# A routed expert layer on one core: VectorE's loop without a placed head, and forty increments ahead of TensorE's stream

## The chip, the cores and the metric

The kernel runs on one core of one Trainium2 chip. The number that counts is the device time of one execution in microseconds (us), from the first instruction of the program to its last wait, as the median of several executions. A profiled execution is one of them with every instruction and DMA packet recorded.

## What is computed

The input is x of 64 batches by 64 channels by 512 (4096 rows, "tokens", of 512). A first product mixes the 64 channels of a batch by a matrix chosen by the batch's subject and adds a bias. The result h goes through a mixture of experts, and the sum is added to x:

```
h      = einsum('bct,bcd->bdt', x, w[subject]) + bias[subject]
scores = sigmoid(h @ gate.T)                 # 16 experts in 4 groups
sel, w = best 4 experts out of the best 2 groups (by scores + expert_bias)
w      = 2.5 * scores[sel] / sum(scores[sel])
out    = sum over the 4 chosen e:  w_e * (silu(h @ g_e.T) * (h @ u_e.T)) @ d_e.T
shared = (silu(h @ gs.T) * (h @ us.T)) @ ds.T
x      = x + out + shared                    # H = 512, inner size I = 256
```

## The kernel before, in words

**Stages.** The rows are cut into 32 tiles of 128. In a first stage TensorE forms h (line 1031, two tiles at a time out of four 64x64 pieces each), turns it (line 982) and forms the gate's logits (line 1008). In the second stage it computes the shared expert for all 32 tiles (lines 1144 to 1171), while VectorE works out the routing: which tokens go to which expert and in which of 143 tiles of 128 slots. In the third stage, the longest, the 143 routed tiles follow each other: GpSimd gathers a tile's rows by an indirect DMA, SyncE's DMAs rearrange them, VectorE transposes them, and TensorE does twelve matmuls into psGU (gate and up), two transposes of the product of the tile before, and six matmuls into psY (down) of the tile before that (function step, line 1215). Every weight and activation is split into a high and a low fp32r part, so a product is three matmuls. ScalarE takes the silu and the high parts, VectorE the mix by the routing weight (line 1758) and the low parts (lines 1749 and 1677), ScalarE copies psY out, and GpSimd scatters it, adding to the output.

**What sets the order.** Each engine has its own list of instructions, written out by hand, and engines meet only at semaphores. For the routed tiles every engine but GpSimd has a loop, built by the function run_tiles: some tiles written out ahead of the loop (head), a loop whose body holds 16 tiles, and some written out behind it (tail). TensorE and ScalarE (the tuple FFN) have 13 tiles ahead, eight turns and 2 tiles behind; VectorE and SyncE (the tuple EARLY) have 16 ahead, seven turns and 15 behind. All loops ask for a hint on their closing branch, which is given at the top of each turn.

**TensorE's beginning.** It waits for two memsets, runs eight warm-up matmuls on a tile of ones (line 968), waits for the constants (line 969) and goes on with the first pair of h tiles and the bias. A similar device, semaphore increments that nobody waits for, stands in SyncE's list (SP_STEPS, lines 502 and 503).

Of the kernel before, what the change touches and what calls it, by code (L numbers as in the profile page):

```python
# [83 lines left out]
GROUP = 4  # L84
RAW_LOADS = {15: 1, 16: 2, 23: 3, 31: 4}
WARM_UP = 8
DVE_HEAD = 77
SP_STEPS = 6
N_PAIRS = NT // 2
LATE_CONSTS = range(3, 8)  # L90
EIGHT = 8
# [28 lines left out]
def tile_at(n):  # L120
    return Tile(n // RING, n % RING)

def run_tiles(eng, first, head, rounds, tail, step, slot=None):

    for n in range(first, first + head):
        step(tile_at(n), n, n - first)
    start = first + head
    unroll = 2  # L130
    with eng.bass.Fori(0, rounds // unroll, engines=[eng.engine], hint_back_edge=True,
                      head_slot=None if slot is None else {eng.engine: slot}) as turn:
        for j in range(unroll * RING):
            step(Tile(turn * unroll + (start + j) // RING, (start + j) % RING), None, j)
    start += RING * rounds
    for n in range(start, start + tail):
        step(tile_at(n), n, n - start)

def build(nc, x, x_pairs, itok, fside, cond_w, gate_w, expert_bias, ffn_w, out):  # L140
# [4 lines left out]
    with ExitStack() as ctx:  # L145
# [6 lines left out]
        def sem(name):  # L152
            return ctx.enter_context(nc.semaphore(name))
# [134 lines left out]
        first = in_x([E, NRP])  # L288
# [85 lines left out]
        pads_cleared = sem("pads_cleared")  # L374
        scatter_ok = sem("scatter_ok")
        sp_clear = sem("sp_clear")
        act_clear = sem("act_clear")
        dve_clear = sem("dve_clear")
        shuffled = [sem(f"shuffled{s}") for s in range(RING // DUO_TILES)]
# [15 lines left out]
        EARLY = (NT, 2 * RING, TURNS - 2, NR - RING * TURNS)  # L395
# [101 lines left out]
        def _(sp):  # L497
# [3 lines left out]
            sp.dma_start(fside2[:], fside).then_inc(fside_loaded, 16)  # L501
            for _ in range(SP_STEPS):
                sp.sem_inc(sp_clear, 1)
# [5 lines left out]

            for m in range(N_PAIRS):  # L510
                if m + X_PAIRS < N_PAIRS:
                    sp.wait_ge(cond_done, 2 * (m + 1))
# [89 lines left out]
            for n in range(NT):  # L602
                step(tile_at(n), n, n)
            run_tiles(sp, *EARLY, step)
            for s in range(YRING):
                sp.wait_ge(scattered[s], 16 * ((NT + NR + YRING - 1 - s) // YRING))

        @block.gpsimd
        def _(pool):
# [50 lines left out]
            word = None  # L660
            for m in range(N_PAIRS):
                if m == 1:
# [69 lines left out]
        def _(act):  # L732
# [42 lines left out]
            def copy_h(n):  # L775
                act.wait_ge(cond_done, n + 1)
                if n >= H_RING:
                    act.wait_ge(h_stored[n % H_RING], n // H_RING * 16)
                    act.wait_ge(a_xposed, n + 1 - H_RING)
                act.activation(h_row(n), h_bank(n)[:], ACT.Identity,  # L780
                               bias=bias_tok[:, n:n + 1]).then_inc(h_ready, 1)

            def keep_xT(n):
                if n == DVE_COPIES:
                    act.wait_ge(a_xT_ready, DVE_COPIES)
                act.wait_ge(a_xposed, n + 1)
                act.activation(kept_xT(n), psT[n % 2][:], ACT.Copy).then_inc(a_xT_ready, 1)
# [6 lines left out]

            for m in range(N_PAIRS + 1):
                pair = (2 * m, 2 * m + 1)
                if m < N_PAIRS:
                    for n in pair:
                        copy_h(n)
                if m == N_PAIRS:  # L800
                    keep_xT(NT - 2)
# [151 lines left out]
            for n in range(NT):  # L953
                shared_step(n)
            run_tiles(act, *FFN, step)
            act.wait_ge(down_done, LAST - 1)
            for k in range(IK):
# [7 lines left out]
        def _(pe):  # L965
            pe.wait_ge(blank, 2)
            for _ in range(WARM_UP):
                pe.matmul(psM[:, 0:P], ones[:], ones[:], start=True, stop=True)  # L968
            pe.wait_ge(consts, 1)

            def bias():
# [270 lines left out]
            def last_downs(w, last_w):  # L1242
# [19 lines left out]
                mm.then_inc(down_done, 1)  # L1262

            run_tiles(pe, *FFN, step)
            last_downs(kept[-2], kept[-1])

        @block.vector
        def _(v):
# [173 lines left out]
            used, not_last, start, end, turn, prep, prep_end = [e_rows[:, k, :] for k in range(7)]  # L1442
# [263 lines left out]
            def shared_step(n):  # L1706

                g, part = divmod(n, GROUP)
                more = g < NT // GROUP - 1
                if part == 0:  # L1710
                    if g > 0:
                        shared_mix(g - 1, 1)
                    else:
                        route_part(n)
                    if more:
                        split_shared_x(GROUP * (g + 1))
                    if g > 0:
                        split_shared_hid(g - 1, 0)
                        split_shared_hid(g - 1, 1)
                elif part == 1:  # L1720
                    if more:
                        split_shared_x(GROUP * (g + 1) + 1)
                    if g == 0:
                        route_part(n)
                    shared_mix(g, 0)
                elif part == 2 and more:
                    split_shared_x(GROUP * (g + 1) + 2)
                    split_shared_x(GROUP * (g + 1) + 3)
                if n > 1:
                    route_part(n)  # L1730
                if n in LOWS:
                    split_low(*LOWS[n])
                if n == NT - 2:
                    turn_x(tile_at(NT))
                elif n == NT - 1:
                    split_x(tile_at(NT))
                    turn_x(tile_at(NT + 1))
# [153 lines left out]
            first_word = []  # L1891
            for n in range(NT):
                shared_step(n)
            run_tiles(v, *EARLY, step, DVE_HEAD)
            for k in range(IK):
                v.wait_ge(hidhi_ready, LAST + 1 + k)
                v.tensor_tensor(last_hidT(hidT_lo, k), last_hid_bank(k), last_hidT(hidT_hi, k).bitcast(F32), ALU.subtract
# [48 lines left out]
```

## Time and profile before

| | |
|---|---|
| three executions | 825.04, 826.39, 826.95 us; median 826.39 |
| profiled execution, its own time | 826.33 us |
| its span, first to last instruction | 824.5 us |
| TensorE busy | 812.5 us, 99% |
| VectorE, ScalarE, GpSimd busy | 485.0, 388.3, 433.4 us |
| fetch queue of TensorE (q8) | 17 packets, 0.28 MB |
| fetch queue of the other engines (q14) | 150 packets, 1.23 MB |

In the profile PE is TensorE, PEld its weight loads, DVE VectorE, ACT ScalarE, POOL GpSimd and SP SyncE; a letter q behind a name is that engine's instruction queue (registers, branches, semaphores), whose work is not counted as busy. Matmuls are pipelined: the shown duration of one is longer than the distance to the next, so groups are compared by their starts. In a row of the timeline the brackets hold the idle time of the engine ahead of the group and what ended it; "issue" there means that nothing the profile shows was waited for. fp32 matmuls run as two passes and count twice.

### The profile page before, as it was taken

To read this page: it belongs to the slowest core of one execution; us is meant where nothing else is said; L and a number is where in the kernel's file an instruction comes from. 1 tells how busy PE (TensorE), PEld (TensorE's weight loads), DVE (VectorE), ACT (ScalarE), POOL (GpSimd) and SP (SyncE) were. 2 spreads that over 40 slices of the span, in tenths; PEclk is the share of its full clock that TensorE was granted. 3 is DMA by queue.
4 is the path that set the end of the run, shared out by engine and by line. 5 is a ranking of instruction groups with operands and counts; after the bars stand their busy time and mean duration, and the time that the engine had idled before them with its cause. 6 is when DMAs were issued, how large, how long until landed. Compare 5 with 4: busy or idle time off the path is not lost.

```text
span 824.5 us, 19365 instructions
## 1 busy us (share of the span) xinstructions
PE 812.5 (99%) x4133; PEld 649.7 (79%) x4134; DVE 485.0 (59%) x1017; ACT 388.3 (47%) x782; POOL 433.4 (53%) x399
## 2 busy tenths in 40 slices
PE   9999999999999999999999999999999999999996
PEld 5578778888887888888888888888888888888874
DVE  5798899627444446644457446647557466464441
ACT  4864334535334345534455445546455355453441
POOL 5403112625567555566665665655565573765543
PEclk9999999999999999999999999999999999999999
DMA  8986969899999899899997999899998998998965
GB/s 288 394 332 177 247 149 260 204 203 268 239 251 237 177 192 176 202 276 241 182 196 185 270 216 217 210 267 189 229 266 175 282 246 198 236 206 164 198 94 68
DMA packets 145305, 181.52 MB, mean 220 GB/s; under 512 B 30570, under 2 KB 103922, under 8 KB 142834
## 3 DMA queue, kind: packets, MB, share of 16 engines
q0 software_dynamic: 37776, 89.08, 52.3%
q1 hardware_dynamic: 106528, 80.45, 38.4%
q10 hardware_dynamic: 834, 10.49, 3.6%
q14 instruction: 150, 1.23, 0.5%
q8 instruction: 17, 0.28, 0.1%
HBM read 82.52 MB, written 67.17 MB: 182 GB/s over the span
## 4 chain that ended last, share of the span: by engine, by line
PE 93%; DVE 3%; issue 1%; DMA 1%; ACT 1%; POOLq 0%; POOL 0%; DVEq 0%; SPq 0%; ACTq 0%
PE psGU L1111 47%; PE psY L1111 23%; PE psY L1169 5%; PE psH L982 4%; PE psGU L1152 3%; PE psGU L1154 3%; PE psGU L1153 3%; PE psT L982 1%; DMA raw_w<-ffn_w 1%; PE psY L1031 1%; PE psGU L1031 1%; PE psH L1008 1%; PE psM L1139 1%; PE psM L968 0%; DVE aT_low L1703 0%
## 5 line engine op out<-in xcount | busy, mean ns | idle before, releaser
L1111 PE MATMUL psGU<-split_w,xT_pair 128*128 x1716 | 415.9, 391 | 1.0 <-issue 1.0
L1111 PEld LDWEIGHTS psGU<-split_w,xT_pair 128*128 128x128 f32 x1716 | 321.9, 188 | 71.7 <-issue 1.9
L694 POOL DMA_INDIRECT out<-y_ring,idx_all x143 | 228.8, 1600 | 203.6 <-SPq L583 184.1
L1758 DVE SCALAR_TENSOR_TENSOR aT<-aT,w_ring,psGU 128x256 f32<-128x256 f32 x143 | 68.6, 480 | 238.6 <-ACT aT L934 216.1
L689 POOL DMA_INDIRECT tok_ring<-h_rows,idx_all x143 | 150.3, 1051 | 73.3 <-issue 42.0
L1111 PE MATMUL psY<-split_w,hidT_hi 128*128 x564 | 187.9, 414 | 0.0
L934 ACT ACTIVATE aT<-psGU 128x256 f32<-128x256 f32 x143 | 55.0, 384 | 255.2 <-PE psGU L1111 255.2
L840 ACT ACTIVATE y_ring<-psY 128x512 f32<-128x512 f32 x173 | 103.6, 599 | 101.1 <-PE psY L1111 63.3
L1111 PE MATMUL psY<-split_w,hidT_lo 128*128 x282 | 111.4, 395 | 0.0
L1111 PEld LDWEIGHTS psY<-split_w,hidT_hi 128*128 128x128 f32 x564 | 95.4, 189 | 13.5 <-issue 0.2
L1743 DVE STREAM_TRANSPOSE psT<-x_ring 128x512 f32<-128x512 f32 x143 | 102.5, 717 | 0.1
L1677 DVE TENSOR_TENSOR xT_pair<-psT,xT_pair 128x512 fp32r<-128x512 f32 x143 | 97.4, 681 | 4.7 <-issue 2.6
L755 ACT ACTIVATE xT_pair<-psT 128x512 fp32r<-128x512 f32 x143 | 86.3, 604 | 0.8 <-DVE psT L1743 0.8
L702 POOL DMA_DIRECT2D out<-y_ring x32 | 29.6, 1169 | 91.4 <-ACT y_ring L840 90.1
L1771 DVE TENSOR_TENSOR split_w<-raw_w,split_w x42 | 51.5, 1226 | 33.3 <-ACT split_w L906 31.7
L1111 PEld LDWEIGHTS psY<-split_w,hidT_lo 128*128 128x128 f32 x282 | 52.8, 187 | 12.4
L1749 DVE TENSOR_TENSOR hidT_lo<-psH,hidT_hi 128x256 fp32r<-128x256 f32 x142 | 59.3, 417 | 4.0 <-ACT hidT_hi L831 4.0
L831 ACT ACTIVATE hidT_hi<-psH 128x256 fp32r<-128x256 f32 x142 | 53.8, 379 | 1.6 <-PE psH L982 1.6
L982 PE MATMUL psH<-ident,aT 128*128 128x128 f32 x284 | 54.0, 272 | 0.5 <-DVE hidT_lo L1749 0.5
L982 PEld LDWEIGHTS psH<-ident,aT 128*128 128x128 f32 x284 | 39.3, 139 | 19.2 <-DVE aT L1758 0.9
L906 ACT ACTIVATE split_w<-raw_w x42 | 44.6, 1061 | 7.3 <-issue 2.4
L1153 PE MATMUL psGU<-split_w 128*128 128x512 f32 x96 | 37.4, 390 | 0.0
(268 smaller groups left out, 651.4 us busy)
## 6 DMA issues: line engine op xcount, KB each, us to landing
x_ring<-tok_ring SPq DMA_DIRECT2D x284, 128.0 KB
raw_w<-ffn_w SPq DMA_DIRECT2D x17, 1536.0 KB, 10.1
out<-y_ring POOLq DMA_DIRECT2D x32, 256.0 KB, 7.5
x_ring<-x_pairs SPq DMA_DIRECT2D x12, 512.0 KB, 8.6
h_rows<-tok_ring SPq DMA_DIRECT2D x16, 256.0 KB, 9.7
h_rows<-y_ring SPq DMA_DIRECT2D x16, 256.0 KB, 10.0
tok_ring<-h_rows,idx_all POOLq DMA_INDIRECT x143, 6.5
out<-y_ring,idx_all POOLq DMA_INDIRECT x143, 6.2
```

The lines of the kernel that those rows point to most:

```text
L689: pool.indirect_dma_start(tok_ring[:, r % RING, :], None, h_rows[:, :], bass.IndirectOffsetOnAxis(idx_all[:, r:r + 1], 0)).then_inc(gather ...
L694: pool.indirect_dma_start(out[:, :], bass.IndirectOffsetOnAxis(idx_all[:, r:r + 1], 0), y_ring[:, r % YRING, :], None, compute_op=ALU.add) ...
L755: act.activation(xT_hi[:, t.slot % 2, :], psT[t.slot % 2][:], ACT.Copy).then_inc(xhi_ready, 1)
L840: act.activation(y_ring[:, s, :], psY[t.slot % 2][:], ACT.Copy).then_inc(y_ready, 1)
L934: act.activation(silu[:, t.slot % 2, :], psGU[t.slot % 2][:, 0:I], ACT.Silu).then_inc(silu_ready, 1)
L982: mm = pe.transpose(dst[:, k * P:(k + 1) * P], src[:, k * P:(k + 1) * P], ident[:])
L1111: mm = pe.matmul(dst, a[:, slot, c], w(at + col + k * H), start=(k == 0 and a is high and at == 0), stop=(k == parts - 1 and a is low))
L1153: pe.matmul(as_low, split_w[:, w:w + P], low, start=False, stop=False)
L1677: v.tensor_tensor(xT_lo[:, t.slot % 2, :], psT[t.slot % 2][:], xT_hi[:, t.slot % 2, :].bitcast(F32), ALU.subtract).then_inc(xT_ready, 1)
L1743: v.transpose(psT[t.slot % 2][:].rearrange("p (k b j) -> p k j b", k=HK, j=QUADS), x_duo[:, t.slot // DUO_TILES, :, t.slot % DUO_TILES, :] ...
L1749: v.tensor_tensor(hidT_lo[:, t.slot % 2, :], psH[:, 0:I], hidT_hi[:, t.slot % 2, :].bitcast(F32), ALU.subtract).then_inc(hidT_ready, 1)
L1758: v.scalar_tensor_tensor(out=hid[:, half, :], in0=gate, scalar=w_ring[:, w_slot, bass.ds(expert, 1)], in1=up, op0=ALU.mult, op1=ALU.mult). ...
```

## The change

Two edits. The loop of VectorE is built without a slot, so the align instruction ahead of it is gone and its body begins where the code ahead of it ends. And TensorE, behind its warm-up matmuls and ahead of the wait for the constants, increments a new semaphore pe_clear forty times; no engine waits for it. That puts every later instruction of TensorE forty places further, its loop and tail included.

```diff
@@ -84,8 +84,8 @@
 GROUP = 4
 RAW_LOADS = {15: 1, 16: 2, 23: 3, 31: 4}
 WARM_UP = 8
-DVE_HEAD = 77
 SP_STEPS = 6
+PE_STEPS = 40
 N_PAIRS = NT // 2
 LATE_CONSTS = range(3, 8)
 EIGHT = 8
@@ -121,15 +121,14 @@
     return Tile(n // RING, n % RING)
 
 
-def run_tiles(eng, first, head, rounds, tail, step, slot=None):
+def run_tiles(eng, first, head, rounds, tail, step):
 
 
     for n in range(first, first + head):
         step(tile_at(n), n, n - first)
     start = first + head
     unroll = 2
-    with eng.bass.Fori(0, rounds // unroll, engines=[eng.engine], hint_back_edge=True,
-                      head_slot=None if slot is None else {eng.engine: slot}) as turn:
+    with eng.bass.Fori(0, rounds // unroll, engines=[eng.engine], hint_back_edge=True) as turn:
         for j in range(unroll * RING):
             step(Tile(turn * unroll + (start + j) // RING, (start + j) % RING), None, j)
     start += RING * rounds
@@ -374,6 +373,7 @@
         pads_cleared = sem("pads_cleared")
         scatter_ok = sem("scatter_ok")
         sp_clear = sem("sp_clear")
+        pe_clear = sem("pe_clear")
         act_clear = sem("act_clear")
         dve_clear = sem("dve_clear")
         shuffled = [sem(f"shuffled{s}") for s in range(RING // DUO_TILES)]
@@ -966,6 +966,8 @@
             pe.wait_ge(blank, 2)
             for _ in range(WARM_UP):
                 pe.matmul(psM[:, 0:P], ones[:], ones[:], start=True, stop=True)
+            for _ in range(PE_STEPS):
+                pe.sem_inc(pe_clear, 1)
             pe.wait_ge(consts, 1)
 
             def bias():
@@ -1891,7 +1893,7 @@
             first_word = []
             for n in range(NT):
                 shared_step(n)
-            run_tiles(v, *EARLY, step, DVE_HEAD)
+            run_tiles(v, *EARLY, step)
             for k in range(IK):
                 v.wait_ge(hidhi_ready, LAST + 1 + k)
                 v.tensor_tensor(last_hidT(hidT_lo, k), last_hid_bank(k), last_hidT(hidT_hi, k).bitcast(F32), ALU.subtract
```

On VectorE, at the end of the tiles written out ahead of the loop; the ISA row of line 131 is the align instruction, then come the branch into the loop, the hint at the body's top and the body's first instructions. Before:

```order
722 L1778 UNCONDITIONAL_BRANCH
723 L1776 UNCONDITIONAL_BRANCH
724 L1773 UNCONDITIONAL_BRANCH
725 L131 ISA
726 L131 UNCONDITIONAL_BRANCH
727 L131 BRANCH_PREFETCH_HINT
728 L131 ISA
729 L1836 REGISTER_ALU
730 L1836 TENSOR_LOAD words
```

The same place with the change, where lines are two higher from line 969 on:

```order
722 L1780 UNCONDITIONAL_BRANCH
723 L1778 UNCONDITIONAL_BRANCH
724 L1775 UNCONDITIONAL_BRANCH
725 L131 UNCONDITIONAL_BRANCH
726 L131 BRANCH_PREFETCH_HINT
727 L131 ISA
728 L1838 REGISTER_ALU
729 L1838 TENSOR_LOAD words
```

One instruction is gone, and nothing else moved. On TensorE no instruction changes its place among the others: this listing does not show instructions that only touch semaphores, and the forty increments stand between the warm-up and the first product of line 1031.

## Rows read from the trace of the kernel before

**Rows 1.** The page: busy us (share) xinstructions of each engine, and the granted clock.

```profile
PE 812.5 (99%) x4133; PEld 649.7 (79%) x4134; DVE 485.0 (59%) x1017; ACT 388.3 (47%) x782; POOL 433.4 (53%) x399
...
PEclk9999999999999999999999999999999999999999
```

**Rows 2.** Waits of TensorE: us in total, times, longest.

```profile
PE psGU L1111 <- issue: 1.0, 2, 0.7
```

**Rows 3.** Timeline, TensorE: start us, us, engine, line, operation, count [idle before <-releaser].

```profile
244.99 2.91 PE L1111 MATMUL psGU<-split_w,xT_pair 128*128 x12
...
262.40 2.90 PE L1111 MATMUL psGU<-split_w,xT_pair 128*128 x12
265.84 0.41 PE L982 MATMUL psH<-ident,aT 128*128 128x128 f32 x2 [0.53 <-DVE hidT_lo L1749]
...
268.02 3.00 PE L1111 MATMUL psGU<-split_w,xT_pair 128*128 x12 [0.31 <-issue]
...
272.47 2.91 PE L1111 MATMUL psGU<-split_w,xT_pair 128*128 x12
```

**Rows 4.** The same view at the last turn of the loop.

```profile
799.22 2.91 PE L1111 MATMUL psGU<-split_w,xT_pair 128*128 x12
...
804.44 3.02 PE L1111 MATMUL psGU<-split_w,xT_pair 128*128 x12 [0.70 <-issue]
```

**Rows 5.** Line 131, the loop: queue, instruction, count, ns min/median/max, first to last start us.

```profile
L131 PEldq BRANCH_PREFETCH_HINT  x8: 31/31/45, 241.6 to 731.3; - x8
...
L131 PEldq COMPARE_BRANCH  x8: 88/223/257, 312.5 to 800.1; - x8
...
L131 DVEq BRANCH_PREFETCH_HINT  x7: 39/45/61, 263.9 to 681.4; - x7
...
L131 SPq BRANCH_PREFETCH_HINT  x7: 45/51/57, 268.5 to 700.7; - x7
...
L131 PEldq MOVE  x1: 33/33/33, 241.5 to 241.5; - x1
...
L131 DVEq MOVE  x1: 43/43/43, 258.3 to 258.3; - x1
L131 SPq MOVE  x1: 29/29/29, 268.4 to 268.4; - x1
```

**Rows 6.** Timeline, VectorE, around its entry to the loop.

```profile
257.24 0.48 DVE L1758 SCALAR_TENSOR_TENSOR aT<-aT,w_ring,psGU 128x256 f32<-128x256 f32 x1 [2.31 <-ACT aT L934]
...
264.88 0.48 DVE L1758 SCALAR_TENSOR_TENSOR aT<-aT,w_ring,psGU 128x256 f32<-128x256 f32 x1 [5.59 <-issue]
```

**Rows 7.** Instruction queues: packets, MB, share; stretches 0 to 280, 280 to 800, 802 to 806.

```profile
q8 instruction: 15, 0.25, 0.4%
...
q14 instruction: 121, 0.99, 0.6%
...
q8 instruction: 1, 0.02, 1.7%
```

**Rows 8.** Timeline, TensorE, the first ten us.

```profile
1.27 3.78 PE L968 MATMUL psM<-ones 128*128 128x128 f32 x16 [1.27 <-DVE ones L1305]
5.04 1.75 PE L1031 MATMUL psY<-x_ring,cw_ring 64*64 64x512 f32 x8
6.72 0.63 PE L976 MATMUL psH<-subj1h,fside 8*128 8x32 f32 x4
7.32 1.09 PE L1031 MATMUL psGU<-x_ring,cw_ring 64*64 64x512 f32 x8
8.57 1.23 PE L982 MATMUL psT<-ident,tok_ring 128*128 128x128 f32 x8 [0.16 <-ACT tok_ring L780]
```

**Rows 9.** Lines 503 (SyncE) and 1211 (TensorE), in the form of rows 5.

```profile
L503 SPq EVENT_SEMAPHORE  x6: 17/17/17, 2.0 to 2.4; - x6
...
L1211 PEldq EVENT_SEMAPHORE  x1: 51/51/51, 181.9 to 181.9; - x1
```

**Rows 10.** Timeline, GpSimd, the last scatter but one.

```profile
816.28 1.56 POOL L694 DMA_INDIRECT out<-y_ring,idx_all  x1 [2.84 <-SPq L583]
```

## The prediction

> **What bounds the kernel now.** Read first the busy line of the page: TensorE works 812.5 of 824.5 us [rows 1]. The list of TensorE's own waits then says how little there is to win by speed elsewhere: within the tiles the largest is 1.0 us in two pieces put down to "issue" [rows 2]. Third, TensorE's timeline through the routed tiles: a tile is twelve psGU matmuls, two transposes and six psY matmuls, and the psGU groups at 244.99 and 262.40 lie four periods of 4.353 us apart. From 272.47 to 799.22 there are 121 periods in 526.75 us, 4.353 us each, so over seven loop turns nothing on any other engine reaches TensorE [rows 3, 4]. The kernel's time is therefore TensorE's own work plus the few places where its stream breaks, and the change touches three of them: VectorE's entry to its loop, the end of TensorE's loop, and TensorE's first matmuls.
>
> **Part one: VectorE enters its loop without a placed slot.** The loop's own instructions stand on one line for all engines. VectorE sets its counter there at 258.3 and runs the first instruction of the body at 263.9; TensorE does the same at 241.5 and 241.6, SyncE at 268.4 and 268.5 [rows 5]. Of these only VectorE's loop has a placed head, and only VectorE stands still for 5.6 us. In its timeline that is the 5.59 us ahead of the multiply at 264.88 for which "issue" is named, nothing it waits for [rows 6]. 
>
> What it costs TensorE: groups at 266.75 and 271.11 would follow from the period; they come at 268.02 and 272.47 [rows 3]. TensorE first stands 0.53 us for VectorE's split and then 0.31 us before psGU, and its emptied queue adds the rest. The loss is 272.47 - 262.40 - 2 x 4.353 = 1.36 us. The other 4.2 us of VectorE's pause lie under its ordinary slack: it sits idle 2.3 us of a tile [rows 6] and works two tiles ahead on the transposes.
>
> Without the slot the align instruction and the filling go and the body follows the code ahead of it, as on SyncE and TensorE, whose entries take 0.1 us [rows 5]. Gain 1.36 us. Bounds: 0 (the code is late by falling in as well) to 1.36. I take 1.36, by the two entries of the same kind. The body may also lie differently in the blocks. Counting the built program, the natural place is one slot behind the placed one if the preamble is the one that VectorE's pauses at block ends suggest (about 0.4 us every 128 instructions); 77 or 78 then makes no difference. If the count is wrong, other instructions meet a block's end; at 0.4 us against 2.3 us of idle time that is covered. What is late next at tile 48 is nothing: TensorE's wait goes whole, as the release chain there runs through VectorE alone.
>
> The Trainium skill says in "Runtime: NRT & Kernel Launch", section "Instruction fetch mechanics", that prefetch is purely sequential and that a taken branch to a page outside the resident window forces a fetch before execution goes on. The 5.6 us pause agrees with it; by this rule a fall-through entry costs nothing.
>
> **Part two: TensorE's loop and tail move by forty instructions.** TensorE's instruction queue (q8) moved 15 blocks of 16 KB by 280 us, none from 277 to 800, and one in 802 to 806 us, after the last turn, whose closing branch is at 800.1 [rows 5, 7]. The psGU group due at 799.22 + 4.353 = 803.57 starts at 804.44 with 0.70 us put down to "issue" [rows 4]. So the code behind the loop was not there when the loop ended: 0.87 us lost. Counted in the built program, loop and tail are 1109 instructions from 3333 on; the pause lies three instructions into the tail, so a block of 256 ends there. Forty more instructions ahead move the tail's beginning 36 slots into the next block, whose first 36 hold the loop's last instructions and so are fetched in the first turn; the tail's 156 instructions then end before that block does. Gain 0.87 us. Bounds: 0 (another block end meets the tail) and 0.87. I take 0.87. The extra straight-line code ahead of the loop crosses blocks as before, hidden by the sequencer's lead: it stands at the loop's head at 241.6 while the first matmul of that tile starts at 244.99 [rows 3, 5].
>
> **Part three: the increments themselves.** They stand on TensorE's queue between eight warm-up matmuls and the wait for the constants, with the first cond product, the bias product and everything after queued behind. Nobody waits on the new semaphore. Warm-up runs from 1.27 to 5.05, the first cond matmul starts at 5.04, so any delay here is a delay of all [rows 8]. An increment on TensorE runs ahead of the array: the one of line 1211 is done at 181.9, when the shared products still stream [rows 9]. So the forty begin when the 32 issued instructions of the warm-up are out, about 2 us. Price of one: SyncE's six take 2.0 to 2.4, at most 0.08 us apart; TensorE's semaphore instructions take 51 ns where SyncE's take 17 [rows 9], and its own instructions at the loop's head come 0.1 us apart [rows 5]. Forty by 0.08 is 3.2 us, until 5.2; forty by 0.1 is 4.0 us, until 6.0. The nearer row is TensorE's own, so the first cond matmul starts at 6.0, 0.95 us late.
>
> Not all of it stays. The first cond group took 1.75 us and the same group later 1.09 [rows 8]: the array was still in its slow pace until about 6 us. Started at 6.0 it can run at the later pace and end at 7.1, where it ended at 6.79 before: 0.3 us late. The bias, VectorE's two copies and ScalarE's copy (1.22 us from 7.35 to 8.57) follow at the same distance. Cost between 0.2 us (increments as on SyncE) and 3.6 us (if they had to wait for the last warm-up matmul at 4.62, against [rows 9]). I take 0.5 us, between 0.3 and 0.95.
>
> On the pace: the page gives a granted clock of 0.9 or more, the 2.4 GHz level, in every slice from the first on, but the first cond group takes 1.6 times as long as the second [rows 1, 8]. The Trainium skill ("TensorE: Matmul & The Clock Gate", Part 1) says that the array's default state is throttled and that activity releases the throttle; the two groups agree with it, the row of the granted clock does not show it. This rule speaks against the change, since idle time is put in just where the release is due. It is a rival below, priced from rows.
>
> **Sum.** -1.36 - 0.87 + 0.5 = -1.73 us, against the profiled execution's own 826.33 us: 824.6 us. That run is at the median of the runs shown (826.39), so nothing is added. The tail keeps what is won: from the last psGU group the chain runs through TensorE, ScalarE, SyncE and the last two scatters, and GpSimd stands idle 2.84 us before the scatter at 816.28 [rows 10], so earlier matmuls mean an earlier end.
>
> **Rivals.**
> The slow pace lasts longer: with TensorE idle from 5.05 to 6.0, the first cond group stays at 1.75 us and psGU and the transposes behind it pay as much more (0.66 each). Start cost 0.95 + 0.66 + 0.66 = 2.3 us, total +0.04: 826.4. For it speaks that the warm-up is there at all and the slow passes; against it that the idle stretch is short. Chance 0.19.
> The increments are nearly free (0.2 us or less, as SyncE's rows allow): 824.3 or somewhat below. Chance 0.14.
> The entry stall stays, because the body's first block is late even by falling in, or takes a new place: then only 0.87 is won and 0.5 paid, 826.0. Against it, the entries of the two other engines. Chance 0.09.
> Slower: TensorE's loop of 953 instructions lay in four blocks of 256 and now lies in five. If the engine keeps only four, every turn fetches again what it has dropped, and q8 does not stay silent. A missing block cost 0.87 us at the loop's end; seven closing branches are 6.1 us, and 0.87 of the gain is gone: 826.33 + 6.1 - 1.36 + 0.5 = 831.6. From four kept blocks it decides, at five it is nothing. The trace shows only that four are kept. The other engines' queue (q14) moves 121 blocks of 8 KB from 280 to 800 us, 16 per turn [rows 7], so there loops are fetched again each turn, and it mostly hides. Chance 0.07.
> The Trainium skill's same section on instruction fetch gives TensorE 2048 instructions, eight such blocks, by which this rival is dead; no run so far shows it.
> The forecast itself, 823.9 to 825.5: 0.51.
>
> **How the numbers follow.** 0.2% is 1.65 us here, about what a measurement tells from no change, and the forecast of -1.73 lies on that line: of its 0.51 I give 0.33 to faster and 0.18 to the same. The nearly free increments add 0.13 to faster. The slow pace and the kept stall are the same but for 0.05. Slower: the five blocks and what is left of long starts. Faster 0.46, same 0.43, slower 0.11. Range 823.6 to 826.9, which leaves out the five blocks and the upper bound of the start.
>
> **What would show it.** VectorE's counter and first instruction of the body on the loop's line 0.1 us apart at about 258, no "issue" idle of 5.6 us, and psGU groups in one unbroken period from 201 on. A last-turn psGU on the period, and q8 with its last packet before 320 us. Forty TensorE increments ending near 6 us and the first transposes some 0.5 us later than 8.57. Wrong would be q8 packets in every turn, an idle TensorE near 258 to 272, or a first cond group later than 6.5 us.

## The result

The changed kernel is slower. Its median over 22 executions is 828.95 us (827.76 to 832.49), that of the kernel before over as many 826.16 us (823.01 to 831.06). The ratio is 1.0039, 95% interval 1.0029 to 1.0049: 2.4 to 4.0 us more, where 1.7 us less was forecast. The profiled execution took 829.97 us with a span of 828.2 us.

The page's busy line and clock row after. TensorE works 1.8 us longer on the same number of matmuls than in [rows 1], and the last digit of the clock row is an 8:

```profile
PE 814.3 (98%) x4133; PEld 650.6 (79%) x4134; DVE 484.4 (58%) x1017; ACT 388.2 (47%) x782; POOL 435.9 (53%) x399
...
PEclk8999999999999999999999999999999999999998
```

TensorE's timeline of the first 18 us, in the form of [rows 8]:

```profile
1.27 3.67 PE L968 MATMUL psM<-ones 128*128 128x128 f32 x16 [1.27 <-DVE ones L1307]
7.54 1.50 PE L1033 MATMUL psY<-x_ring,cw_ring 64*64 64x512 f32 x8 [2.61 <-POOL cw_ring L678]
8.97 1.06 PE L978 MATMUL psH<-subj1h,fside 8*128 8x32 f32 x4
9.96 1.98 PE L1033 MATMUL psGU<-x_ring,cw_ring 64*64 64x512 f32 x8
11.88 1.97 PE L984 MATMUL psT<-ident,tok_ring 128*128 128x128 f32 x8
...
16.36 1.09 PE L1033 MATMUL psGU<-x_ring,cw_ring 64*64 64x512 f32 x8
```

The first product comes at 7.54, 2.50 us later than before, and the groups behind it, which ran at 1.09 us before, need 1.98 and 1.97 until some 15 us. By 16.36 the kernel is 4.58 us behind; the same group in the timeline of the kernel before:

```profile
11.78 1.09 PE L1031 MATMUL psGU<-x_ring,cw_ring 64*64 64x512 f32 x8
```

The release named in the bracket, a copy of GpSimd, had long been there; TensorE stood behind its own increments. They are one row of their line (form of [rows 9]):

```profile
L970 PEldq EVENT_SEMAPHORE  x40: 51/51/51, 1.3 to 7.3; - x40
```

Forty in 6.0 us are 0.15 us each (the commonest distance between two is 0.151), though a record is 51 ns long. And the clock by short stretches (stretch, length, busy time and count of the five engines, granted clock, DMA share, GB/s):

```profile
7.50:8.00 0.50, 0.46 (x5) 0.24 (x8) 0.00 (x0) 0.00 (x0) 0.38 (x3) 1.00 0.89 287
8.00:8.50 0.50, 0.50 (x8) 0.00 (x0) 0.00 (x0) 0.00 (x0) 0.26 (x2) 0.60 0.83 328
...
14.00:14.50 0.50, 0.50 (x4) 0.07 (x4) 0.50 (x1) 0.00 (x0) 0.00 (x0) 0.50 0.98 401
14.50:15.00 0.50, 0.50 (x8) 0.00 (x0) 0.07 (x1) 0.00 (x0) 0.00 (x0) 0.57 0.45 180
15.00:15.50 0.50, 0.50 (x5) 0.17 (x2) 0.00 (x0) 0.05 (x1) 0.00 (x0) 1.00 0.00 0
```

0.50 is the 1.2 GHz level. The mixed values 0.60 and 0.57 put its beginning at 8.1 and its end at 14.9, after an array that stood idle from 4.93 to 7.54. The first group, with 1.50 us, lies across the fall: it began at the upper level and ended at the lower one.

The two places that were to be won are won. VectorE's entry and the end of TensorE's loop, in the forms of [rows 5] and [rows 4]; VectorE sets its counter and runs the hint at the head of the body in the same tenth, and the psGU groups of the last turn are one period apart:

```profile
L131 DVEq BRANCH_PREFETCH_HINT  x7: 39/45/61, 262.6 to 686.4; - x7
...
L131 DVEq MOVE  x1: 43/43/43, 262.6 to 262.6; - x1
```

```profile
804.11 2.91 PE L1113 MATMUL psGU<-split_w,xT_pair 128*128 x12
808.46 2.91 PE L1113 MATMUL psGU<-split_w,xT_pair 128*128 x12
```

But the 121 unbroken periods of [rows 3] have a break now, far from both edits. TensorE, then VectorE, near 680 us:

```profile
675.90 2.90 PE L1113 MATMUL psGU<-split_w,xT_pair 128*128 x12
680.00 0.41 PE L984 MATMUL psH<-ident,aT 128*128 128x128 f32 x2 [1.20 <-DVE hidT_lo L1751]
...
682.09 3.03 PE L1113 MATMUL psGU<-split_w,xT_pair 128*128 x12 [0.21 <-issue]
686.57 2.91 PE L1113 MATMUL psGU<-split_w,xT_pair 128*128 x12
```

```profile
676.47 0.73 DVE L1745 STREAM_TRANSPOSE psT<-x_ring 128x512 f32<-128x512 f32 x1 [3.87 <-DMA w_ring<-tok_ring]
```

VectorE waited 3.9 us for a tile's rows, and TensorE lost 686.57 - 675.90 - 2 x 4.353 = 1.96 us.

So between the two profiled executions: the group at 244.99 in [rows 3] comes at 249.28, +4.29; entry -1.36; the break near 680 +1.96; end of the loop -0.87; sum +4.02, against 829.97 - 826.33 = 3.64 measured (0.14 of the rest is a shorter step in the tail, about 0.2 lies behind the last matmul). The medians differ by 2.8, and the ratio of 1.0039 is 3.2 us.

### The profile page after: what moved, and what is told of

The parts are those of the page before. It is cut to its first block, busy times and chain, and to the rows that moved or that the text cites. A ratio compares the mean times of both kernels' runs of the same rounds, so it can differ in the third digit from the quotient of the medians.

```text
span 828.2 us, 19404 instructions
## 1 busy us (share of the span) xinstructions
PE 814.3 (98%) x4133; PEld 650.6 (79%) x4134; DVE 484.4 (58%) x1017; ACT 388.2 (47%) x782; POOL 435.9 (53%) x399
## 4 chain that ended last, share of the span: by engine, by line
PE 91%; DVE 2%; DMA 2%; issue 1%; SPq 1%; POOLq 0%; ACT 0%; POOL 0%; DVEq 0%; ACTq 0%
PE psGU L1113 45%; PE psY L1113 23%; PE psY L1171 5%; PE psH L984 4%; PE psGU L1154 3%; PE psGU L1156 3%; PE psGU L1155 3%; PE psT L984 2%; DMA w_ring<-tok_ring 1%; PE psY L1033 1%; PE psGU L1033 1%; PE psH L1010 1%; SPq L544 1%; PE psM L1141 1%; DVE aT_low L1705 0%
```

## The experiments

Each is timed against executions of the kernel before on its own chip; e1 to e4, e5 to e8 and e9 to e12 ran on three different chips, so kernels of different groups are compared by their ratios. The table reads the profiled execution of each in the same way: how much later (+) than in [rows 3] the psGU group of 244.99 comes, which is the cost of the beginning, and what TensorE lost against the period of 4.353 us at VectorE's entry, in the loop, and at the end of its own loop. It is one execution of each: the kernels with at most seven increments, where nothing is expected at the beginning, spread there from -0.57 to +1.78. A loss counts as it occurs, though in e3, e9 and e10 the periods behind the last one are up to 0.03 us shorter and give some of it back.

| kernel | ratio (95%) | beginning | entry | in the loop | end |
|---|---|---|---|---|---|
| before | 1 | 0 | 1.36 | 0 | 0.87 |
| changed | 1.0039 (1.0029 to 1.0049) | +4.29 | 0 | 1.96 | 0 |
| e1 slot gone | 0.9998 (0.9981 to 1.0014) | -0.57 | 0 | 0.22 | 1.13 |
| e2 forty, slot kept | 1.0024 (1.0007 to 1.0041) | +5.91 | 0 | 0.27 and 1.27 | 0 |
| e3 sixteen | 0.9974 (0.9955 to 0.9992) | +1.40 | 0 | 0.53 | 0 |
| e4 forty, 14 warm-up | 1.0066 (1.0040 to 1.0092) | +7.59 | 0 | 1.22 | 0 |
| e5 forty among 20 warm-up | 1.0021 (1.0012 to 1.0030) | +2.66 | 0 | 0 | 0 |
| e6 forty, spread later | 0.9993 (0.9972 to 1.0014) | +1.37 | 0 | 0 | 0 |
| e7 seven | 0.9989 (0.9980 to 0.9999) | -0.14 | 0 | 0.88 | 0 |
| e8 three | one execution | -0.10 | 0 | 0 | 1.63 |
| e9 slot 100 | 1.0008 (0.9986 to 1.0030) | +0.18 | 0 | 1.26 | 1.41 |
| e10 seven, slot kept | 0.9975 (0.9957 to 0.9994) | +1.78 | 1.33 | 1.66 | 0 |
| e11 twenty-eight | 0.9991 (0.9975 to 1.0007) | +3.50 | 0 | 0 | 0 |
| e12 seven once more | 0.9985 (0.9968 to 1.0002) | +0.19 | 0 | 0.61 | 0 |

### One edit each: e1 and e2

```diff
-            run_tiles(v, *EARLY, step, DVE_HEAD)
+            run_tiles(v, *EARLY, step)
```

> The kernel before with VectorE's slot alone taken away. Theory: VectorE's entry to its loop takes 0.1 us instead of 5.5, TensorE's waits at 265.8 and 268.0 go, all else stays: 1.36 us less, ratio 0.9984; the start is as before (first product of the channel mix at 5.0 us, granted clock 1.00), the 0.87 us at the end of TensorE's loop stay. Rival: without the slot VectorE's body lies so that a late transfer meets TensorE, and the wait of 1.2 us near 680 us seen in the changed kernel is here as well; then the gain is used up, ratio 1.0000.

Measured 0.9998. The trace does what the theory says: counter and hint at 257.8 and 257.9, no loss at the entry, no break near 680 of the size feared (0.22). But the time does not show 1.36 us. The interval still holds the theory's 0.9984 and does not decide; what speaks against 1.36 in the mean is e2.

```diff
+            for _ in range(PE_STEPS):            # 40
+                pe.sem_inc(pe_clear, 1)
```

> The kernel before with the forty increments alone. Theory: they take 0.151 us each from 1.34 to 7.3, TensorE stands idle from 5.0 to 7.5, its granted clock falls to 0.5 from about 8.2 to 14.5; start cost 4.3 us, end of the loop 0.87 won: 3.4 us more, ratio 1.0042. VectorE's entry costs 1.36 as before. If the 1.2 us wait near 680 comes from these increments (everything being later against the transfers), it is here too and the ratio is 1.0058; if it comes from VectorE's edit, it isn't. Rival for the start: the clock falls only together with VectorE's edit, which nothing at the start speaks for; then the cost is 2.5 and the ratio 1.0020.

Measured 1.0024: the rival's 1.0020 lies in the interval, the theory's 1.0042 just outside it. The time alone would speak for the rival, but the trace shows its premise false, for the slow pace is there without VectorE's edit. TensorE's warm-up and first groups in e2:

```profile
1.27 3.78 PE L970 MATMUL psM<-ones 128*128 128x128 f32 x16 [1.27 <-DVE ones L1309]
7.54 1.99 PE L1035 MATMUL psY<-x_ring,cw_ring 64*64 64x512 f32 x8 [2.50 <-POOL cw_ring L680]
9.46 1.06 PE L980 MATMUL psH<-subj1h,fside 8*128 8x32 f32 x4
10.45 1.98 PE L1035 MATMUL psGU<-x_ring,cw_ring 64*64 64x512 f32 x8
```

The same 2.50 us of idle array and the same half pace, without VectorE's edit. One thing differs. The first group takes 1.99 us, all at the lower level, where it took 1.50 in the changed kernel, and the sixteen warm-up passes took 3.78 us, where they took 3.67. So here the array had not reached the upper level before it ran dry, and it first got there at 16.6 us: the level did not fall, its first rise was put off. The clock row says 1.00 all this time, for the trace has no record of the clock ahead of that rise; the pace of the groups is the witness.

The 22 executions of the changed kernel fall into two groups. Nine have a mean clock of 0.993 or 0.994, as the profiled one, the other thirteen 0.997 to 0.999, as the profiled e2, and their medians are 828.9 and 829.0 us. That the thirteen are of e2's kind is not shown, only one of the 22 having a trace, but they are as slow.

VectorE's entry, with the slot in place, cost TensorE nothing in e2. The loop's line for VectorE, and TensorE's groups around it:

```profile
L132 DVEq BRANCH_PREFETCH_HINT  x7: 39/45/56, 270.0 to 687.5; - x7
...
L132 DVEq MOVE  x1: 43/43/43, 265.5 to 265.5; - x1
```

```profile
260.77 3.02 PE L1115 MATMUL psGU<-split_w,xT_pair 128*128 x12 [0.23 <-issue]
265.23 2.91 PE L1115 MATMUL psGU<-split_w,xT_pair 128*128 x12
269.58 2.91 PE L1115 MATMUL psGU<-split_w,xT_pair 128*128 x12
```

VectorE's pause is there, 4.5 us, yet 265.23 to 269.58 is one period. ScalarE had paused for 3.96 us at 251.7 to 255.7; this cost TensorE 1.27 us then. After it VectorE did the mixes of two tiles 2.2 us apart (at 262.24 and 264.42, a half period), and I take it that this lead covered its own pause. The 1.36 us of the kernel before is thus one draw, not a constant.

### Fewer increments: e3, e11

```diff
-PE_STEPS = 40
+PE_STEPS = 16      # e11: 28
```

> The changed kernel with 16 increments instead of 40. Theory: 16 x 0.151 = 2.4 us, they are done at 3.8, before the warm-up ends at 5.05; the first product of the channel mix starts at 5.04, clock 1.00, no start cost. Sixteen still put the first instruction of the tail 12 slots behind a block end, in one block with the loop's last ones: 0.87 won; entry 1.36 won. 2.2 us less than before, ratio 0.9973. Rival: the start cost comes from the shift of TensorE's code against its blocks and is in proportion, 16/40 of 4.3 = 1.7 us: ratio 0.9994, with idle time between 5 and 48 us.

Measured 0.9974: faster than both kernels, beside the theory's 0.9973. Since the gain at VectorE's entry shows in no other time, part of this agreement may be luck. The rival is wrong on the place (no increment stood in the way: they ended at 3.7), but the beginning was 1.40 us late in the profiled execution all the same:

```profile
5.57 1.09 PE L1033 MATMUL psY<-x_ring,cw_ring 64*64 64x512 f32 x8 [0.70 <-issue]
...
7.81 1.89 PE L1033 MATMUL psGU<-x_ring,cw_ring 64*64 64x512 f32 x8 [0.60 <-DMA x_ring<-x_pairs]
9.64 1.92 PE L984 MATMUL psT<-ident,tok_ring 128*128 128x128 f32 x8
```

```profile
8.00:9.00 1.00, 1.00 (x8) 0.03 (x3) 0.00 (x0) 0.96 (x2) 0.65 (x4) 0.50 0.98 373
```

The wait for the first x tile ended at 5.5, where it ended at 5.0 before, and a second one came at 7.2; after 1.3 us of idle time in two pieces the granted clock fell here too, from 8.0 to 11.4. The kernel before seems to know this: of its 93 executions in these comparisons 11 had a mean clock of 0.996 or less, with a median of 829.8 us, the other 82 one of 826.0. No trace shows one of the 11.

> The changed kernel with 28 increments. They end at 1.34 + 28 x 0.151 = 5.6 us, the first product starts at 5.8, 0.75 us later than before, the array stands idle for 0.8 us. Theory: beside the 0.75 the granted clock may fall in some executions, as it did with sixteen after idle stretches of 0.70 and 0.60; start cost 0.75 to 3.5 us, against 4.3 to 5.9 with forty. Ratio 0.9985 to 1.0005. Rival (the cost is in proportion to the number): 28/40 of 4.3 to 5.9 = 3.0 to 4.1 us, ratio 1.0010 to 1.0025.

Measured 0.9991. The first product came at 5.73 as expected, 0.69 us behind the warm-up, and its group took 1.98 us at once:

```profile
5.73 1.98 PE L1033 MATMUL psY<-x_ring,cw_ring 64*64 64x512 f32 x8 [0.69 <-POOL cw_ring L678]
7.65 1.05 PE L978 MATMUL psH<-subj1h,fside 8*128 8x32 f32 x4
8.63 1.99 PE L1033 MATMUL psGU<-x_ring,cw_ring 64*64 64x512 f32 x8
```

The cost of the beginning, 3.50 us, is within both expectations; the ratio is within the theory's, and its interval (to 1.0007) ends below the rival's. As in e2, the array had not reached its full pace when the warm-up ended, and it got there only at 14.1 us. So 0.69 us of idle array was enough for that in this execution; the ratio hints that not every execution pays as much.

### Late, but never idle: e4, e5

```diff
-WARM_UP = 8
+WARM_UP = 14
```

> The changed kernel with 14 warm-up matmuls instead of 8. Six more of 0.427 us keep the array busy until 7.6 us, past the last increment. Theory (the clock falls because the array stood idle): granted clock stays 1.00, the first product starts at 7.6 and its group is as fast as the later ones (1.09); start cost 2.0 to 2.5 us instead of 4.3: ratio 0.9998 to 1.0004. Rival (the clock falls for another reason, such as the later start itself): clock 0.5 for some 6 us as in the changed kernel, ratio 1.0025 or more.

Measured 1.0066, the worst of all. The theory's numbers missed, since their premise did: the six matmuls did not cover the increments, they put them off.

```profile
1.27 5.30 PE L968 MATMUL psM<-ones 128*128 128x128 f32 x28 [1.27 <-DVE ones L1307]
9.82 1.99 PE L1033 MATMUL psY<-x_ring,cw_ring 64*64 64x512 f32 x8 [3.25 <-POOL cw_ring L678]
```

```profile
L970 PEldq EVENT_SEMAPHORE  x40: 51/51/51, 3.6 to 9.6; - x40
```

The first increment runs at 3.58, when the weights of the twelfth of the 28 passes have started (3.57) and its matmul has not (3.78). A pass is two instructions (weights and matmul): 56 less 23 are 33, or 32 if the matmul that waits for its weights is not counted. TensorE's sequencer runs at most that far ahead here; the 16 passes of eight matmuls are 32, no more than that, and the increments of the changed kernel start at 1.34. The idle stretch grew to 3.25 us. In it, at 8.7, the granted clock fell, and the slow pace lasted to 18.9 us. So this run did not hold the array busy and did not test what it was made for; e5 does. But it shows the other half: here the array had come to the upper level at 5.3 (the last nine passes are 0.112 us apart) and lost it by standing idle. All six executions have a mean clock of 0.992 to 0.994.

```diff
-WARM_UP = 8
+WARM_UP = 20
             for _ in range(WARM_UP):
                 pe.matmul(psM[:, 0:P], ones[:], ones[:], start=True, stop=True)
-            for _ in range(PE_STEPS):
-                pe.sem_inc(pe_clear, 1)
+                for _ in range(PE_STEPS // WARM_UP):
+                    pe.sem_inc(pe_clear, 1)
```

> The changed kernel with 20 warm-up matmuls and the forty increments dealt out between them, two behind each, so that the array has work all the time until the last increment. At 0.213 us a pass for the first 18 and 0.112 for the other 22 the warm-up ends at 7.6 us, about as late as the increments do in the changed kernel (7.54). Theory (what idleness costs): same late start, but no idle array, so the groups behind it run at 1.0 to 1.1 us instead of 1.5 to 2.0; the first gate product after 48 us comes 2.0 us later than before where it came 4.3 later in the changed kernel; ratio 1.0000 (0.9990 to 1.0010). Rival (the late start itself, or the increments, slow the array): groups of 1.9 us for some 6 us as in the changed kernel, ratio 1.0035.

```profile
1.26 7.50 PE L968 MATMUL psM<-ones 128*128 128x128 f32 x40 [1.26 <-DVE ones L1307]
8.70 1.09 PE L1033 MATMUL psY<-x_ring,cw_ring 64*64 64x512 f32 x8
9.71 0.63 PE L978 MATMUL psH<-subj1h,fside 8*128 8x32 f32 x4
10.27 1.09 PE L1033 MATMUL psGU<-x_ring,cw_ring 64*64 64x512 f32 x8
```

The first product is at 8.70, 1.16 us later than in the changed kernel (the passes ran 0.213 us apart until 7.15, not to about 5 as I had reckoned), and yet the beginning costs 2.66 us instead of 4.29: every group behind it takes 1.09 or 0.63. Measured 1.0021 against 1.0039. Start late without idling and there is no half pace; the mean clock of all twelve executions is 0.997 or 0.998, where nine of the changed kernel's 22 were below. The theory of idleness holds. The ratio is above the expected band: 0.66 us of that is the longer warm-up, and the rest is about what the band counted for VectorE's entry, 1.36 us that the times do not show (2.66 - 0.87 = 1.8 us, a ratio of 1.0022, an estimate from the two profiles).

### Forty where the queue is full: e6

```diff
+                if n in (6, 10, 14, 18, 22):
+                    for _ in range(PE_STEPS // 5):
+                        pe.sem_inc(pe_clear, 1)
```

(behind the steps of the shared expert; those at the beginning are gone)

> The changed kernel with its forty increments taken from the beginning and put, eight each, behind five steps of the shared expert (n = 6, 10, 14, 18, 22), where TensorE has products queued. Theory: 8 x 0.151 = 1.2 us is less than the sequencer's lead there, so they cost nothing; beginning as before, no pause at the end of TensorE's loop: 0.87 to 1.1 won there, and 0 to 1.36 at VectorE's entry. Ratio 0.9974 to 0.9990. Rival (increments cost 6 us of TensorE's path wherever they stand): idle time of 1.2 us in each of the five steps, ratio above 1.003.

Measured 0.9993, a little above the expected band and far from the rival. Nowhere between 60 and 150 us does TensorE stand still for more than 0.17 us: forty increments cost nothing when the queue holds work. The pause at the loop's end is gone here too. The beginning was 1.37 us late in this execution for waits on x transfers (0.99 us at 28.9), not on increments. By the times it cannot be told from seven at the beginning.

### Where the block ends: e7, e8 and e12

```diff
-PE_STEPS = 40
+PE_STEPS = 7       # e8: 3
```

> The changed kernel with 7 increments. They end at 2.4 us, under the warm-up, so the beginning is as before. Theory of the blocks: the tail begins 3 instructions behind a block's end, in one block with the loop's last three, so nothing has to be loaded when the loop ends: no pause there. Ratio as with sixteen, 0.997. Rival (a few instructions are not enough since the load is asked for earlier than it is used, or the count of the block is off): a pause of 0.9 us or more remains at about 802 us.

> The changed kernel with 3 increments, a look only. Theory of the blocks: the tail begins one instruction ahead of a block's end, so nearly all of it lies in a block that is not there when the loop ends: the pause at the end of TensorE's loop is back, 0.9 us or somewhat more, and TensorE's queue loads a block at about 800 us whose arrival ends it. Rival (any shift helps): no pause.

TensorE's groups at the end of the loop, of e7 and then of e8:

```profile
798.59 2.91 PE L1113 MATMUL psGU<-split_w,xT_pair 128*128 x12
802.95 2.91 PE L1113 MATMUL psGU<-split_w,xT_pair 128*128 x12
```

```profile
797.76 2.91 PE L1113 MATMUL psGU<-split_w,xT_pair 128*128 x12
803.75 3.04 PE L1113 MATMUL psGU<-split_w,xT_pair 128*128 x12 [1.46 <-issue]
```

Four instructions decide between nothing and 1.63 us (803.75 - 797.76 - 4.353). With three the queue q8 loads a block from 800.50 to 801.88 and another at 805.39; with seven its only late block, at 801.90, is the one behind the tail, and nobody waits. The count by blocks holds within these four instructions. e7 is 0.9989 (0.9980 to 0.9999), which misses the expected 0.997: the pause is gone, but less is won than I had added up. e12, the same kernel again, beside e10, is 0.9985:

> The changed kernel with 7 increments once more, beside the one that has seven increments and the slot. Theory: both pauses gone, beginning as before; ratio 0.9975 to 0.9990, faster than both kernels, and 0 to 1.4 us faster than seven increments with the slot.

### What makes VectorE's entry slow: e9 and e10

```diff
-DVE_HEAD = 77
+DVE_HEAD = 100
```

> The kernel before with VectorE's loop at slot 100 instead of 77, no increments. Theory (the entry waits because the branch goes over a filling of 255 instructions into code not yet loaded): counted in the built program the natural place is 78, so the filling is 22 instructions and the body's first one lies in the same block of 128 as the branch ahead of it; entry 0.1 to 0.5 us instead of 4.5 to 5.5, TensorE not held there; ratio 0.9985 to 1.0000, as with the slot gone. Rival (the align instruction itself, or any branch over filling, costs the 5 us): the pause of 4.5 us or more stays.

```profile
L131 DVEq BRANCH_PREFETCH_HINT  x7: 45/45/61, 258.7 to 681.2; - x7
...
L131 DVEq MOVE  x1: 43/43/43, 258.5 to 258.5; - x1
```

0.2 us with the align instruction and a branch in place. So neither of these makes the entry slow, but where the branch goes: over a filling of 255 instructions or of 22, by the count in the built program. The instruction queue q14, which serves all engines but TensorE, agrees. In each of the three executions with a slow entry it moves one block inside the pause, and the body starts 1.5 to 1.7 us after it has landed: 261.99 to 262.32 in the kernel before (pause 258.3 to 263.9), 268.10 to 268.42 in e2 (265.5 to 270.0), 263.84 to 264.54 in e10 (260.7 to 266.2). In e9 it moves none from 255 to 262, nor in the changed kernel from 259 to 265. For which engine a block is the trace does not say. The time is not better for it: 1.0008, interval 0.9986 to 1.0030, above the expected band, which the interval overlaps.

e10 is the kernel before with seven increments and slot 77 kept (the edit of e2, with 7).

> The kernel before with seven increments at TensorE's beginning alone; VectorE's slot of 77 stays. Theory: no pause at the end of TensorE's loop (0.9 to 1.1 us won), VectorE's entry pause of 4.5 to 5.5 us stays and holds TensorE between 0 and 1.4 us, depending on how far VectorE happens to be ahead. Ratio 0.9990 (0.9985 to 1.0000). Against the same without the slot it is 0 to 1.4 us slower. Rival (the entry pause is hidden on the whole): no difference between the two.

```profile
L132 DVEq BRANCH_PREFETCH_HINT  x7: 39/45/56, 266.2 to 683.9; - x7
...
L132 DVEq MOVE  x1: 43/43/43, 260.7 to 260.7; - x1
```

```profile
268.15 0.41 PE L986 MATMUL psH<-ident,aT 128*128 128x128 f32 x2 [1.08 <-DVE hidT_lo L1753]
```

The pause of 5.4 us is there and cost TensorE 1.33 us in this execution; still its ratio is 0.9975 (0.9957 to 0.9994), below the expected 0.9985, and its median, 824.67 us over 12 executions, lies 0.5 us below that of e12 (825.21). The trace speaks for the theory, the times for the rival: on the whole the slot cannot be told from no slot. The best that came out are the kernels with seven or sixteen increments, with and without the slot: 0.9974 to 0.9989 against the kernel before, by their ratios 0.5 to 0.65% below the changed one. What they share is the end of TensorE's loop.

## Why the prediction was wrong

**The step that failed is part three, the cost of the beginning: 0.5 us in the sum, 4.29 measured.** It failed in two places, the price of an increment and the pace behind them. I took 0.1 us for one, from the distance of TensorE's own instructions at the loop's head; it is 0.151. I let them begin at about 2 us; they begin at 1.34, since the 32 instructions of the eight matmuls are no more than the sequencer may be ahead. The two errors went against each other, and the last one started at 7.3, where I had the end at 6.0: the first product 2.50 us late where I had 0.95. The 51 ns of [rows 9] are a duration and not a price per instruction, as the 0.151 us between two increments show. The Trainium skill says in "Perfetto Trace Analysis", section "Per-engine timelines", that the profiler reports only the execution of a sequencer instruction; its drawing puts the push of the semaphore behind that, still on the sequencer. The two figures agree with it.

**"Not all of it stays" had the wrong sign.** I reckoned that a later start finds a faster array and takes about half a microsecond off. That would need an array that goes on working. It stood idle for 2.6 us, and the clock granted fell to 0.5 and stayed there to 14.9 us: 2.50 late became 4.58 by 16.36. This is the rival "the slow pace lasts longer", to which I gave 0.19 and a price of 2.3 us for the whole of the start; its mechanism is right and its size, 4.29 here and 5.91 in e2, is nearly double and more. I let it end with the transposes because [rows 8] shows the array at full pace by 8.57; but the clock that had fallen stayed down for 6.8 us, with the array busy. e5 shows that it is the idleness and not the lateness; e2 and e11 show that an array that runs dry before it has ever reached the upper level stays slow as well, to 16.6 and 14.1 us. The rule in the Trainium skill ("TensorE: Matmul & The Clock Gate", Part 1), that the default is throttled and activity releases it, was the better guide, and I had read it as a rule for the warm-up alone.

One slip in the chances: by the shares given, the same adds up to 0.42 and slower to 0.12, where the text has 0.43 and 0.11.

**Part one: right in the trace, and not in the time.** The entry takes 0.1 us, by the mechanism told (e9, and the block that q14 moves inside each pause), and the execution shown had 1.36 us to win. With the slot in place three executions were profiled: it cost 1.36, 0 and 1.33 us. What I left out is that VectorE's lead over TensorE at that moment is not the same each time, so a pause of 5 us is worth anything from nothing to 1.36; the sum took the 1.36 of one execution as if it were fixed. Neither e1 nor e10 against e12 shows a gain that can be measured.

**Part two: right.** 0.87 us in the profile of before, 1.13 and 1.41 in two others, none in any kernel with 7 to 40 increments, 1.63 with three. The rival of the five blocks is dead: in the changed kernel q8 loads nothing between 300 and 795 us, so TensorE keeps a loop of 953 instructions that lies in five blocks by the count.

**What no edit made.** Losses in the loop of 0 to 1.96 us appear in most profiled executions, with and without either edit, mostly near 670 to 680 us, where in the changed kernel a tile's rows came late. They are as large as what was to be won, and they hide effects of 1 us. In the changed kernel's profile it is 1.96, and this execution is 1.0 us above its median. What decides when they come was not tried, nor what decides when the array first reaches its full pace.

## What to carry to other kernels

An instruction that only touches a semaphore is cheap only behind a full queue: forty of them cost nothing in the middle of the program and over 4 us at its beginning, where the array ran dry and the clock fell. To shift code by a few instructions, count to the block's end and take as few as do it (seven here), and put them where the engine has work queued. And price a stall on a helper engine by what it does to the bound engine in several executions, not in one.

## What the hardware showed that I had not expected

- TensorE's semaphore increments come 0.151 us apart, also while matmuls run; the records are 51 ns.
- The sequencer was at most 32 or 33 instructions ahead of the array's weight loads and matmuls (first increment at 3.58 in e4, at 1.34 with eight warm-up matmuls).
- In the changed kernel the 1.2 GHz level came 0.6 us after the restart that followed 2.6 us of idle array, and lasted 6.8 us, though the array was busy all the time. In e4 it came within an idle stretch of 3.25 us, and two idle pieces of 0.70 and 0.60 us were enough once (e3).
- The full pace is first reached at a different time in each execution. Where the array did not run dry before, this was between 4.5 us (e7, whose last two warm-up passes are 0.147 us apart) and 7.4 us (e10, whose first group takes 2.39 us); where it did, 14.1 (e11) and 16.6 us (e2).
- An entry to a loop over 22 instructions of filling takes 0.2 us, over 255 it takes 4.5 to 5.6 us, with one block of instructions moved in it (counts from the built program).
